# One core, a sparse-expert and attention layer: who normalises, who fills constants and who makes the column masks in its two routings

## The reference

```python
x = x + 0.5 * ffn(layernorm(x))
x = x + attn(layernorm(x))        # 16 heads of 8, softmax over 1024 keys
x = x + 0.5 * ffn(layernorm(x))   # the same weights again

def ffn(x):                        # 8 experts, 128 -> 512 -> 128
    indices = argmax(softmax(x @ Wr + br))
    out = 0
    for i in range(8):
        xi = x * (indices == i)
        out = out + (relu(xi @ W1[i] + b1[i]) @ W2[i] + b2[i])
    return out
```

## Time and profile before

| | us |
|---|---|
| median of 3 runs | 999.02 (997.89 to 1002.86) |
| the profiled execution | 1000.25 |
| its span | 998.4 |

### The profile page before, as it was taken

The page is one execution under the profiler, slowest core; times in us unless marked ns, Lnnn a source line. Parts: engine busy times, 40 slices in busy tenths (PEclk is TensorE's granted clock), DMA queues, the critical chain, the costliest instruction groups (busy, mean ns, idle before and its releaser), DMA issues. The chain is left out here.

```text
span 998.4 us, 17986 instructions
## 1 busy us (share of the span) xinstructions
PE 918.1 (92%) x5975; PEld 382.3 (38%) x5975; DVE 829.9 (83%) x1396; ACT 752.1 (75%) x1509; POOL 217.3 (22%) x315
## 2 busy tenths in 40 slices
PE   3789966889999999999999999999999999965996
PEld 2689853422222222222222222222222222434996
DVE  6766558979999999999999999999999998768664
ACT  3367636878888888888888888888888888754774
POOL 5157631841000001000000100000100000024775
PEclk9789988989999999999999999999999999996998
DMA  8624535842220203202022120220202000051321
GB/s 265 184 86 120 160 108 191 257 168 63 63 60 17 62 30 85 61 18 62 15 72 75 31 62 15 72 54 28 75 30 64 30 22 17 1 170 48 104 64 43
DMA packets 68130, 78.67 MB, mean 79 GB/s; under 512 B 13088, under 2 KB 45512, under 8 KB 68040
## 3 DMA queue, kind: packets, MB, share of 16 engines
q1 hardware_dynamic: 61464, 64.52, 22.2%
q0 software_dynamic: 5120, 12.59, 4.1%
q10 hardware_dynamic: 1456, 0.41, 0.2%
HBM read 40.47 MB, written 33.49 MB: 74 GB/s over the span
## 5 line engine op out<-in xcount | busy, mean ns | idle before, releaser
L1561 DVE TENSOR_REDUCE maxima<-ps_m 128x2 f32<-128x1024 f32 x512 | 602.6, 1220 | 58.2 <-PE ps_m L1324 56.3
L1531 ACT ACTIVATE probs<-ps_s 128x512 f32<-128x512 f32 x1024 | 555.9, 599 | 109.1 <-PE ps_s L1370 78.7
L1370 PE MATMUL ps_s<-q,k 74*128 74x512 bf16 (+1 forms) x1024 | 312.1, 386 | 3.0 <-ACT probs L1531 3.0
L1381 PE MATMUL ps_o<-probs,vs 128*32 128x512 f32 x2048 | 273.6, 606 | 0.7 <-ACT probs L1531 0.7
L1370 PEld LDWEIGHTS ps_s<-q,k 74*128 74x128 bf16 (+1 forms) x1024 | 79.6, 97 | 307.1 <-ACT probs L1531 219.1
L1324 PE MATMUL ps_m<-k,q 64*128 64x512 bf16 x1024 | 160.1, 386 | 5.1 <-DVE maxima L1561 4.0
L1254 POOL TENSOR_SCALAR split<-top 128x16 bf16<-128x16 f32 x32 | 8.1, 253 | 443.0 <-DVE top L1577 429.3
L690 PE MATMUL ps_y<-W,hT 128*128 x624 | 86.4, 281 | 3.4 <-DVE hT L846 2.1
L1324 PEld LDWEIGHTS ps_m<-k,q 64*128 64x128 bf16 x1024 | 48.9, 93 | 102.3 <-issue 57.0
L1381 PEld LDWEIGHTS ps_o<-probs,vs 128*32 128x32 f32 x2048 | 40.3, 108 | 109.7 <-issue 94.7
L690 PEld LDWEIGHTS ps_y<-W,hT 128*128 128x128 f32 x624 | 78.1, 195 | 5.3 <-issue 5.1
(11 more groups left out here) (213 smaller groups left out, 571.7 us busy)
## 6 DMA issues: line engine op xcount, KB each, us to landing
k_rows<-parts SPq DMA_DIRECT2D x24, 384.0 KB, 4.4
sums<-oT SPq DMA_DIRECT2D x30, 256.0 KB, 2.1
q<-q_parts SPq DMA_DIRECT2D x75, 96.0 KB
k<-k_rows SPq DMA_DIRECT2D x15, 288.0 KB
token_rows<-x SPq DMA_DIRECT2D x16, 256.0 KB, 3.8
token_rows<-v_and_ctx SPq DMA_DIRECT2D x16, 256.0 KB, 4.1
k<-k_rows SPq DMA_DIRECT2D x15, 256.0 KB
q_parts<-parts SPq DMA_DIRECT2D x8, 384.0 KB, 3.4
```

The costliest lines, as they stand in the source:

```text
L1370: nc.tensor.matmul(ps_s[n % 3][:, :], k2[buffer(g)][0:contracted, j, kt * P:(kt + 1) * P], q2[buffer(g)][0:contracted, j, u * HALF:(u + 1) ...
L1381: last = nc.tensor.matmul(ps_o[32 * j:32 * (j + 1), :], vs[buffer(g)][:, kt, j, :], probs[:, s % 2, j, :], start=(kt == 0), stop=(kt == KT ...
L1531: nc.scalar.activation(probs[:, s % 2, j, :], ps_s[n % 3][:, :], ACT.Exp, scale=SCALE).then_inc(exped, 1)
L1561: nc.vector.tensor_reduce(maxima[:, :, pr, qt, kh], ps_m[slot][:, :, :], AX.X, ALU.max).then_inc(unit_free[slot], 1)
```

## The change

- Front: `BY_ACT` becomes 0, 1, 2 and `BY_POOL` 3, 6; DVE normalises 4, 5, 7. PE's wait for the small loads moves from before its 24 filler turns to before the first logits. Eight more filler turns follow each of turns 0 to 3, and sixteen stand before `count`.
- `EARLY` becomes 6 experts (48 matmuls before `find`, 16 after). ACT's two copies still take four experts each (`BANK`).
- First expert pass: ACT copies the late half before it waits for the item list. DVE does relu(0), `vector_total`, relu(1), `vector_rest`.
- The twelve fills are POOL memsets, the bf16 buffers seen as float (half as many elements), one after each of the first twelve scatters. `blank` and its two memsets are gone, and `units` is half as wide.
- Both routings: POOL makes the column masks of the last four tiles, after `in_tile` is there, and `find` waits for them on POOL's semaphore.
- Second routing: ACT takes the root before the first copy of logits.

```diff
-        self.blank = sb("blank", [P, 2, SEQ], BF16)
-        self.units = sb("units", [P, 2 * P], F32)
+        self.units = sb("units", [P, P], F32)
...
-        nc.gpsimd.memset(self.blank[:, 0, :], 0.0).then_inc(self.made, 1)
-        nc.gpsimd.memset(self.blank[:, 1, :], 1.0).then_inc(self.made, 1)
-
-    FILLED = 16 * 4 * BUFS
-
-    def sync_fill(self, sp):
...
+    FILLED = 4 * BUFS
...
+    def gpsimd_fill(self, pool, n):
+
+        p, piece = n // 4, n % 4
+        if n:
+            pool.wait_ge(self.filled, n)
+        if piece == 0:
+            self.nc.gpsimd.memset(self.k2[p][64:96, 0::2, :].bitcast(F32), self.PAIR).then_inc(self.filled, 1)
+        if piece == 1:
+            self.nc.gpsimd.memset(self.k2[p][0:64, 1::2, :].bitcast(F32), self.PAIR).then_inc(self.filled, 1)
+        if piece == 2:
+            self.nc.gpsimd.memset(self.q2[p][0:64, 1::2, :].bitcast(F32), 0.0).then_inc(self.filled, 1)
+        if piece == 3:
+            self.nc.gpsimd.memset(self.vs[p][:, :, :, :], 1.0).then_inc(self.filled, 1)
...
-        self.small_loaded(pe)
...
-    EARLY = EXPERTS // 2
+    EARLY, BANK = EXPERTS - 2, EXPERTS // 2
...
-    def find(self, pe):
+    def find(self, pe, columns_done, count):
...
-                pe.wait_ge(self.column, t // QUAD + 1)
+                if t < self.BY_POOL:
+                    pe.wait_ge(self.column, t // QUAD + 1)
+                else:
+                    pe.wait_ge(columns_done, count)
...
+    IN_TILE, BY_POOL = 23, TILES - QUAD
+
+    def gpsimd_columns(self, pool, done):
+
+        pool.wait_ge(self.routed, self.IN_TILE)
+        for t in range(self.BY_POOL, TILES):
+            last = self.nc.gpsimd.tensor_scalar(self.columns[:, t, :], self.w["iota_b"][:, :], self.in_tile[:, t:t + 1], None, ALU.is_equal)
+        last.then_inc(done, 1)
...
-        for t in range(TILES):
+        for t in range(self.BY_POOL):
             last = nc.vector.tensor_scalar(self.columns[:, t, :], w["iota_b"][:, :], self.in_tile[:, t:t + 1], None, ALU.is_equal)
...
-    BY_ACT, BY_POOL = (0, 2, QUADS - 1), (1, 3, QUAD + 1)
+    BY_ACT, BY_POOL = (0, 1, 2), (3, QUAD + 2)
...
         normalise(0)
+        normalise(1)
+        self.norm.root(act, (QUAD * QUAD, TILES), 1)
         normalise(2)
-        self.norm.root(act, (QUAD * QUAD, TILES), 1)
         for q in range(QUADS):
-            if q == QUAD:
-                normalise(QUADS - 1)
...
         for q in range(QUAD + 1):
             turn(q)
+            if q < QUAD:
+                self.setup.tensor_turns(pe, self.route.ps_lT, 8)
+        self.setup.small_loaded(pe)
         self.route.logits(pe, 0)
...
+        self.setup.tensor_turns(pe, self.route.ps_lT, 16)
         self.route.count(pe)
         self.setup.tensor_idle(pe)
-        self.route.find(pe)
+        self.route.find(pe, self.normed_pool, len(self.BY_POOL) + 1)
...
+        self.route.gpsimd_columns(pool, self.normed_pool)
         pool.wait_ge(self.route.stored, 2 * 16 * QUADS)
...
             scatter(t)
+            if self.setup and t < self.setup.FILLED:
+                self.setup.gpsimd_fill(pool, t)
...
+        if self.setup:
+            self.setup.scalar_idle_late(act)
         act.wait_ge(self.listed, self.NAMED)
...
         self.list_items(dve)
+        relu(0)
         if self.setup:
             self.setup.vector_total(dve)
-        relu(0)
-        if self.setup:
+            relu(1)
             self.setup.vector_rest(dve)
-        relu(1)
+        else:
+            relu(1)
...
-                tiles.setup.sync_fill(sp)
...
+                route.gpsimd_columns(pool, normed_pool)
...
+                norm_2.root(act, last_span, 1)
                 route.copied_logits(act, 0)
-                norm_2.root(act, last_span, 1)
```

More of the change, by code:

```diff
@@ L180, in gpsimd_masks @@
         nc.gpsimd.memset(self.units[:, :], 1.0).then_inc(self.made, 1)
-        nc.gpsimd.memset(self.blank[:, 0, :], 0.0).then_inc(self.made, 1)
-        nc.gpsimd.memset(self.blank[:, 1, :], 1.0).then_inc(self.made, 1)
-    FILLED = 16 * 4 * BUFS
-    def sync_fill(self, sp):
-        def constant(value, rows):
-            return self.blank[rows, value, :].unsqueeze(1).to_broadcast([rows.stop - rows.start, GH // 2, SEQ])
-        sp.wait_ge(self.made, 12)
-        for p in range(BUFS):
-            sp.dma_start(self.k2[p][64:96, 0::2, :], constant(1, slice(64, 96))).then_inc(self.filled, 16)
-            sp.dma_start(self.k2[p][0:64, 1::2, :], constant(1, slice(0, 64))).then_inc(self.filled, 16)
-            sp.dma_start(self.q2[p][0:64, 1::2, :], constant(0, slice(0, 64))).then_inc(self.filled, 16)
-            sp.dma_start(self.vs[p][:, :, :, :].rearrange("p t j c -> p (t j c)").rearrange("p (a c) -> p a c", c=2 * P),
-                         self.units[:, :].unsqueeze(1).to_broadcast([P, KT * GH * 32 // (2 * P), 2 * P])).then_inc(self.filled, 16)
+    FILLED = 4 * BUFS
+    PAIR = float(0x3f803f80 - 0x3f800000) / 2 ** 23 + 1.0
+    def gpsimd_fill(self, pool, n):
[10 more added lines that the diff above has]
+            self.nc.gpsimd.memset(self.vs[p][:, :, :, :], 1.0).then_inc(self.filled, 1)
     def tensor_biases(self, pe):
@@ L251, in scalar_idle @@
         self.nc.scalar.activation(self.biases[:, :], self.ps_bias[:, 0:D], ACT.Copy).then_inc(self.idle_out, 1)
-        self.nc.scalar.activation(self.idle[:, 0:self.EARLY, :], self.ps_idle[:, 0:self.EARLY, :], ACT.Copy).then_inc(self.idle_out, 1)
+        self.nc.scalar.activation(self.idle[:, 0:self.BANK, :], self.ps_idle[:, 0:self.BANK, :], ACT.Copy).then_inc(self.idle_out, 1)
     def scalar_idle_late(self, act):
         act.wait_ge(self.idle_done, 2)
-        self.nc.scalar.activation(self.idle[:, self.EARLY:, :], self.ps_idle[:, self.EARLY:, :], ACT.Copy).then_inc(self.idle_out, 1)
+        self.nc.scalar.activation(self.idle[:, self.BANK:, :], self.ps_idle[:, self.BANK:, :], ACT.Copy).then_inc(self.idle_out, 1)
     RESTED = 3
@@ L752, in scalar @@
             first.append(weights(i))
-        if self.setup:
-            self.setup.scalar_idle_late(act)
         relu(0)
@@ L1449, in _ @@
                 route.count(pe)
-                route.find(pe)
+                route.find(pe, normed_pool, len(BY_POOL) + 1)
             @block.scalar
```

## The result

| | kernel before | changed kernel |
|---|---|---|
| median | 999.19 us (997.34 to 1002.86) | 1004.18 us (1002.22 to 1005.93) |
| ratio | 1 | 1.0047, 95% interval 1.0031 to 1.0063 |
| profiled execution, span | 1000.25, 998.4 | 1004.86, 1003.0 |

What follows compares the result with a forecast made beforehand. PE busy 92% of the span, attention untouched; at the ends, POOL's queue becomes the first pass's bound. Stage 1.0 plus second routing 0.8 gives 1.8 us off 999.02: 997.2 us, range 992.5 to 1002.8.

Steps and rivals of the forecast that it cites:

- Part 1: Front, first routing: new order of normalising and turns; second choice of experts starts at 28.0, 3.0 us earlier.
- Part 2: First routing: early block of 48 matmuls takes 5.3 us at 2.4 GHz; bounds 0 and +2.9 us.
- rival (b): PE's early block stays at 1.2 GHz, the start gains little: 1000.2 us in all; chance 0.13.
- Part 3: Both routings: POOL makes four column masks in at most 3.2 us, ready before DVE's 28; net gain 0.3 us each.
- rival (c): Shared port makes DVE's and POOL's column masks exclude each other: slower, 1002.8 us in all; chance 0.13.
- Part 4: Start of first expert pass: new order on DVE and ACT gains 2.6 us, bounds 0.5 and 3.
- Part 5: First pass's scatters: twelve POOL fills of 0.90 make POOL the bound; stage gain 1.0 us rather than 5.8.
- slack: POOL's scatters in the kernel before: they ended at 138.4 where 132.4 was possible, so 6.0 us could absorb fills.
- Part 6: Second routing: earlier root and POOL's column masks gain 0.8 us, which goes to the end.
- Cover gone: none: Second routing, in Part 6: claimed that the change takes away no cover there, so 0 us was charged.

## Why the prediction was wrong, step by step

- **Part 1, the front.** Forecast: choice at 28.0, 3.0 earlier. Measured in the profiled pair: 0.94. The x loads of that execution landed later and DVE waited 2.38 us for one. Over nine profiles with the new front (eight from 28.3 to 29.2, and this one, 30.03) and four with the old (30.97 to 31.52), the middle values are 28.9 and 31.4: 2.5. The mechanism was right and the size a bit high; "at most 0.2" for DVE's start was right in the middle (its normalising starts at 17.6 to 19.0, before at 17.8 to 18.3), but left out that a start bound by a landing moves by 1 us from one execution to the next.
- **Part 2, early experts.** 5.3 forecast, 5.62 measured, clock 1.00. Right; rival (b) is out.
- **Part 3, POOL's masks.** Net gain 0.3 forecast (its cast at 41.1 took 0.4 off), 0.25 measured in the first routing (-0.94 became -1.19). Four masks took 3.56 us, above the 3.2 that was given as the most, because the first took 1.52; they were ready before DVE's all the same. DVE lost 0.2 in all, so the lock of rival (c) did not happen: these masks were not held up as DVE's cast was under the memsets (1.44 us, 0.22 in the changed kernel without them). The rule of the Trainium skill ("SBUF — State Buffer", SBUF: two separate sides) names a two-port mode of DVE as the condition for such a block by an operation with one source. If the masks run in one, which no row says, the trace does not agree with the rule here.
- **Part 4, start of the pass.** 2.6 forecast, 3.45 - 1.19 = 2.26 measured, the most of nine profiles (1.5 to 2.3). down(3) at 60.54, for 58.0 forecast; most of the difference is Part 1's.
- **Part 5, the fills.** Right in the queue: 0.90 forecast and 0.84 measured for a fill, POOL the bound, no wait for DVE to the end, scatters at 2.13 then 1.29. Last scatter 136.4 forecast, 138.15 measured, because it starts from the front's lead, 3.45 instead of 5.8. Instead of a gain of 1.0, a loss of 0.6 in this pair. The lead is the term that was sized too large: in the middle of nine new profiles and four old the first scatter is 4.4 ahead, not 5.8. Over the three profiles that run the changed kernel's whole first pass the last scatter starts at 137.55 to 138.15, over the two that run the old one at 137.45 and 138.17, so the gain of 1.0 is not there in any of them. This is the second step that failed: Parts 1 and 4 were sized too large. **Wrong in one sentence: "Twelve DMAs [...] lay beside the scatters and cost no time".** They cost the items 5.8 us of pace, 4 us of the whole. This did not change the sum, since POOL's end set it; but the row that I took as slack (scatters that wait for DVE from 118.04) was the trace of it, and the question why DVE was late there was not asked. It also hid that the end of the items would come at 126.3, and that there was far more to gain from the fills than the move gave.
- **Attention.** Taken as untouched. It began at 1.2 GHz for 4 us longer, 1.0 us, and ended 2.24 behind; 0.7 more came in small steps between 167 and 871. None of this is shown to be the change's. From the first statistics to the start of POOL's normalising in the second routing it took 739.1 us, before 737.4; but over nine profiles with the short start it took 736.4 to 738.1, and over four with the long one 738.6 to 739.1, and kernels with the fills in front are among the four.
- **Part 6, second routing.** 0.8 forecast, 0.62 measured up to the cast (choice 0.41). **"Cover gone: none" is the step that failed, and the largest in this pair.** POOL's masks were priced as four operations against DVE's 28. What stood behind them was not asked: the block's end, where POOL's drain comes 5.4 us after its last operation. 906.7 + 5.4 = 912.1, for a cast at 909.74: 2.1 us, and a pass that begins with PE colder, another 0.9 in the profile (0.6 on average of the four kernels with that wait). The drain of 11.8 us was in the trace of before, at a time when nobody waited.

Together: 1.6 (stage) + 1.0 + 0.7 (attention) + 0.2 + 2.1 + 0.9 = 6.5, and from a forecast of -1.8 that is +4.7; the span grew by 4.6. The median moved by 5.0. This adds up the profiled pair. Of it the drain's 2.1 is shown by experiment; the stage's share was some 0.4 us worse in this pair than in others, and attention's 1.7 can be chance. So it is also luck that the pair adds up to the median. With the masks back on DVE the kernel stood at 1.0027, inside the range, but still slower and not faster: the drain alone does not make the miss. Of the rivals none was the one: (c) named the right sign and nearly the right time for a reason that did not occur.

## What to carry to other kernels

When an edit gives an engine that had been done early something to do late, add what the end of the block costs it (here 5.4 us after POOL's last operation, after one, four and eight of them), and compare the sum with the engine that ends last. When a stage has a stretch in which a queue waits for a compute engine, ask first what slowed that engine: a DMA that "lies beside" the work showed here in the number of matmuls per window, not in any wait on it. And fill work belongs where its engine is idle, not where its queue is the next to be late: the same twelve memsets were worth -4 us in the front and +3.4 us behind the scatters.

## What the runs showed of the hardware that was not expected

- POOL's drain at a block's end took 5.4 us from the end of its last operation, in the same way after one, four and eight tensor_scalar operations. ACT's lasted 4.03, but ended 0.1 after ACT's last operation.
- A POOL tensor_scalar (128x128 bf16, one pointer scalar) took 0.68 to 0.71 us beside DVE's masks, and the first of a row 1.44 to 1.52: it ended 0.5 us after DVE's comparison of 1024 bf16 that had started just before it. DVE's comparison took 1.22 with POOL's mask beside it and without.
- While DMA fills of 128 to 512 KB moved 160 to 286 GB/s, PE's items went at 150 matmuls instead of 205 in 22 us, at a granted clock of 1.00 and with waits that no row names.
- POOL's memsets of 1024 elements (0.94 to 0.98 us, for 32, 64 or 128 partitions) left DVE's operations beside them unchanged (0.29, on 128 floats), while a DVE cast under two of them took 1.44 in the kernel before, and 0.22 in the changed kernel, where they are gone.
- A POOL DMA waits 0.30 behind another DMA, and 0.17 behind a memset.
- The version with the fills in front, the second routing's masks on DVE and the rest of the change was 0.90% faster than the kernel before (0.9910), the best of those run, and level with the same kernel with 20 filler turns ahead of the second pass.
